# A graph layer and 64 routed experts on one core: aggregation turned round, a third output buffer, gate and up products side by side

## What is computed

```python
h = layernorm(x)
agg = segment_sum(h[src], dst)
t = relu(batch_norm(((1 + eps) * h + agg) @ W1 + b1))
x = x + h + relu(batch_norm(t @ W2 + b2))
y = layernorm(x)
shared = sum(swiglu(y, sWg[e], sWu[e], sWd[e]) for e in range(2))
gate = normalised top 6 of softmax(y @ Wr)
routed = sum(swiglu(y, Wg[e], Wu[e], Wd[e]) * gate[:, e:e+1] for e in range(64))
out = x + y + shared + routed
```

## Time and profile before

| | us |
|---|---|
| median of 3 runs (782.78 to 783.72) | 783.21 |
| the profiled execution | 782.4 |
| its span, first to last instruction | 780.7 |
| PE busy (7096 products) | 722.4 |
| DVE busy | 260.5 |
| ACT busy | 195.1 |
| POOL busy | 174.7 |
| HBM read and written, over the span | 301 GB/s |

### The profile page before, as it was taken

How to read it: one execution, slowest core, us unless ns; L and a number is a source line. 1 busy time by engine, 2 the same in 40 slices (tenths; PEclk the granted TensorE clock), 3 DMA queues, 4 the chain that set the end, 5 groups by cost and what they waited for, 6 DMA issues and landing times. The chain is left out here.

```text
span 780.7 us, 17521 instructions
## 1 busy us (share of the span) xinstructions
PE 722.4 (93%) x7096; PEld 478.5 (61%) x7096; DVE 260.5 (33%) x788; ACT 195.1 (25%) x497; POOL 174.7 (22%) x157
## 2 busy tenths in 40 slices
PE   2699999879999999999999999999999999489993
PEld 2597776556666666555566666655566666356662
DVE  7983524975221442222221212121233222012100
ACT  1222321402332222211222222121222333033331
POOL 4000000011222232232332222222333332123211
PEclk9999999999999999999999999999999999789996
DMA  9970021426999999999999999999999999999921
GB/s 265 407 280 3 0 108 62 166 75 222 354 341 337 347 387 382 392 392 380 385 387 390 378 401 377 384 394 389 383 384 372 373 374 368 342 369 364 337 36 23
DMA packets 57265, 236.35 MB, mean 303 GB/s; under 512 B 6171, under 2 KB 6335, under 8 KB 40286
## 3 DMA queue, kind: packets, MB, share of 16 engines
q1 hardware_dynamic: 46004, 211.33, 70.8%
q0 software_dynamic: 10144, 20.56, 11.4%
q10 hardware_dynamic: 1034, 3.30, 1.1%
HBM read 222.32 MB, written 12.83 MB: 301 GB/s over the span
## 5 line engine op out<-in xcount | busy, mean ns | idle before, releaser
L424 POOL DMA_INDIRECT xg<-x_tab,idx_sb x64 | 71.8, 1121 | 387.9 <-DVE idx_sb L942 220.0
L1368 PE MATMUL ps<-ring,xT 128*64 128x256 f32 x1296 | 156.5, 383 | 0.6 <-ACT xT L608 0.6
L439 POOL DMA_INDIRECT out<-ysb,idx_sb x64 | 92.5, 1445 | 202.4 <-DMA out<-ysb,idx_sb 124.4
L1368 PEld LDWEIGHTS ps<-ring,xT 128*64 128x64 f32 x1296 | 88.1, 137 | 43.8 <-issue 3.4
L628 ACT ACTIVATE ysb<-ps 64x256 f32<-64x256 f32 x64 | 24.2, 377 | 332.3 <-PE ps L1368 152.5
L935 DVE TENSOR_REDUCE gates<-ps 128x1 f32<-128x3 f32 (+1 forms) x62 | 10.0, 162 | 267.7 <-PE ps L1275 267.0
L1368 PE MATMUL ps<-ring,hTj 128*64 128x256 f32 x624 | 75.5, 384 | 0.0
L1368 PE MATMUL ps<-w,xT 128*64 128x256 f32 x608 | 75.1, 390 | 0.0
L903 DVE TENSOR_TENSOR onehot<-iotaAB,slotv 125x640 bf16<-125x640 f32 (+1 forms) x64 | 67.3, 1051 | 2.6 <-PE ps L1283 1.8
L999 DVE SCALAR_TENSOR_TENSOR hs<-hs,gates,ps 128x256 f32<-128x256 f32 x64 | 30.7, 480 | 90.2 <-PE ps L1373 43.8
L1368 PEld LDWEIGHTS ps<-ring,hTj 128*64 128x64 f32 x624 | 42.1, 136 | 30.1 <-issue 11.9
(11 more groups left out here) (237 smaller groups left out, 818.2 us busy)
## 6 DMA issues: line engine op xcount, KB each, us to landing
ring<-in_L_ffn_Wg SPq DMA_DIRECT2D x41, 1024.0 KB, 20.7
ring<-in_L_ffn_Wu SPq DMA_DIRECT2D x40, 1024.0 KB, 21.2
ring<-in_L_ffn_Wd SPq DMA_DIRECT2D x39, 1024.0 KB, 22.5
w<-in_L_ffn_Wd SPq DMA_DIRECT2D x20, 1024.0 KB, 22.4
w<-in_L_ffn_Wg SPq DMA_DIRECT2D x19, 1024.0 KB, 21.6
w<-in_L_ffn_Wu SPq DMA_DIRECT2D x19, 1024.0 KB, 21.3
ring_x<-in_L_ffn_Wu SPq DMA_DIRECT2D x5, 1024.0 KB, 20.2
ring_x<-in_L_ffn_Wd SPq DMA_DIRECT2D x5, 1024.0 KB, 20.3
```

The source lines that it names most:

```text
L424: g.indirect_dma_start(out=xg[j % NX][0:ROWS[j], :], out_offset=None, in_=x_tab, in_offset=bass.IndirectOffsetOnAxis(ap=idx_sb[0:ROWS[j], ...
L439: g.indirect_dma_start(out=out, out_offset=bass.IndirectOffsetOnAxis(ap=idx_sb[0:ROWS[j], j:j + 1].bitcast(u32), axis=0), in_=ysb[h][0:ROW ...
L1368: last = t_.matmul(ps[h * BIG:(h + 1) * BIG, bank, 0:AW], big(k), w[:, k, h * AW:(h + 1) * AW], start=(k == 0), stop=(k == KD - 1))
```

## The change

In the graph stage:

- The operands of the aggregation change places: aT is stationary and h0 moving, so a block's result comes out as rows, 125 x 512, in one PSUM bank. Both are of type float32r; h0 is held as a rounded part h0_hi (ACT) and the rest h0_lo (DVE), and both parts are multiplied: 10 products of 512 columns a block.
- at_diag and agg_copy go. Instead DVE computes h rows = (1 + eps) h0 + PSUM (`h_rows`), PE transposes them (4 products), and ACT copies to hT (blocks 0 to 3) or DVE adds onto zeros (block 4).
- The destination column is spread to int16 by ACT, one activation of 125 x 625 a group, up to ten groups ahead (`spread`); DVE's one_m then has int16 in, int16 in and bf16 out.
- The memory for this is that of ring slots 4 to 7, so SP issues the fifth weight tile only when hT is complete.

In the expert stage:

- Three ysb buffers, one semaphore for all scatters; y_copy(j) waits for scatter(j - 3).
- BASE_AFTER is 47.
- For j >= 1 the gate and up products come together, ahead of transposes, slot product and shared unit; for wide positions the four parts are gate 64, up 64, gate 32, up 32. `tiled`, still used for down, has the 32-row part first.
- The slot values of the experts from 6 on are filled in (`fill_slots(FIXED, E)`) ahead of the sort instead of behind it.

```diff
-    BASE_AFTER = 50
+    BASE_AFTER = 47
+    NY = 3
+    NREP = 10
@@ sync
+                if i == 4:
+                    sp.wait_ge(s_hT, T)
@@ gpsimd: scatter
                 pool.wait_ge(s_y, j + 1)
-                if j >= 2:
-                    pool.wait_ge(s_scat[h], j // 2 * 16)
                 if j >= 1:
-                    pool.wait_ge(s_scat[1 - h], (j + 1) // 2 * 16)
+                    pool.wait_ge(s_scat, 16 * j)
@@ scalar
+            def spread(b):
+                for g in range(b * GB, (b + 1) * GB):
+                    if g >= NREP:
+                        act.wait_ge(s_sm, g - NREP + 1)
+                    sc.activation(rep[g % NREP][:], col_m[:, g * U:(g + 1) * U].unsqueeze(2).broadcast_to([P, U, P]),
+                                  ACT.Copy).then_inc(s_rep, 1)
...
             for t in range(T):
+                sc.activation(h0_hi[:, t, :], x_sb[:, t, :], ACT.Identity, bias=negm[:, t:t + 1],
+                              scale=rstd[0:P, t:t + 1]).then_inc(s_hi, 1)
                 sc.activation(h0[:, t, :], x_sb[:, t, :], ACT.Identity, bias=negm[:, t:t + 1],
                               scale=rstd[0:P, t:t + 1]).then_inc(s_h0, 1)
-            act.wait_ge(s_pre, PRE)
             block_copy(1)
+            spread(2)
             for b in range(2, T):
-                agg_copy(b - 2)
+                if b + 1 < T:
+                    spread(b + 1)
                 block_copy(b)
+                if b == 2:
+                    act.wait_ge(s_pre, PRE)
+                hT_copy(b - 2)
+            hT_copy(T - 2)
@@ vector
+                    last = v.tensor_tensor(one_m[slot][:], iota_m[:], rep[g % NREP][:], ALU.is_equal)
...
+            def h_rows(b):
+                dve.wait_ge(s_agg, b + 1)
+                if b >= 2:
+                    dve.wait_ge(s_hrT, b - 1)
+                v.scalar_tensor_tensor(hrow[b % 2][:], h0[:, b, :], eps1[:], ps[0:P, 4 + b % 2, :], ALU.mult,
+                                       ALU.add).then_inc(s_hrow, 1)
+            block_onehots(1)
+            for t in range(T):
+                dve.wait_ge(s_hi, t + 1)
+                dve.wait_ge(s_h0, t + 1)
+                v.tensor_tensor(h0_lo[:, t, :], h0[:, t, :], h0_hi[:, t, :].bitcast(f32), ALU.subtract).then_inc(s_lo, 1)
+            for b in range(2, T):
+                block_onehots(b, 0, 2)
+                h_rows(b - 2)
+                block_onehots(b, 2, GB)
+            h_rows(T - 2)
+            h_rows(T - 1)
@@ tensor
-            def aggregate(from_aT, bank):
-                for d in range(KD):
-                    for s in range(T):
-                        last = t_.matmul(ps[:, bank, d * P:(d + 1) * P], h0[:, s, d * 128:(d + 1) * 128],
-                                         from_aT[:, s, :], start=(s == 0), stop=(s == T - 1))
+            def aggregate(from_aT, bank, done):
+                for s in range(T):
+                    for part in (h0_hi, h0_lo):
+                        last = t_.matmul(ps[0:P, bank, :], from_aT[:, s, :], part[:, s, :],
+                                         start=(s == 0 and part is h0_hi), stop=(s == T - 1 and part is h0_lo))
...
+            block_aggregate(0)
             for b in range(2, T):
-                block_aggregate(b - 2)
                 visits(b)
-            block_aggregate(T - 2)
+                block_transposes(b - 2)
+                block_aggregate(b - 1)
+            block_transposes(T - 2)
             block_aggregate(T - 1)
...
+            def gate_and_up(x, w_gate, w_up, j):
+                last = big_tiles(0, lambda k: x[:, k, 0:BIG], w_gate())
+                if CAPS[j] == BIG:
+                    last.then_inc(s_g, 1)
+                pe.wait_ge(s_mul, j)
+                if CAPS[j] > BIG:
+                    big_tiles(1, lambda k: x[:, k, 0:BIG], w_up())
+                    small_tiles(0, lambda k: x[:, k, BIG:CAP], w_gate()).then_inc(s_g, 1)
+                    small_tiles(1, lambda k: x[:, k, BIG:CAP], w_up()).then_inc(s_u, 1)
+                else:
+                    big_tiles(1, lambda k: x[:, k, 0:BIG], w_up()).then_inc(s_u, 1)
```

More of the change, by code:

```diff
@@ L161, in gnn_moe_kernel @@
         ring_x = rH0.place("ring_x", [128, KD, 512], f32)
-        aT = [rAT.place(f"aT{i}", [P, T, P], f32) for i in range(2)]
+        aT = [rAT.place(f"aT{i}", [P, T, P], f32r) for i in range(2)]
+        iota_m = rAT.place("iota_m", [P, U, P], i16)
+        hrow = [rAT.place(f"hrow{i}", [P, D], f32) for i in range(2)]
+        rep = [rAT.place("rep0", [P, U, P], i16)]
         rAT.rewind()
@@ L199, in gnn_moe_kernel @@
         hTj = rWin.place("hTj", [128, HW], f32)
-        ysb = [rWin.place(f"ysb{i}", [CAP, D], f32) for i in range(2)]
+        ysb = [rWin.place(f"ysb{i}", [CAP, D], f32) for i in range(NY)]
         perm = rWin.place("perm", [E, E], f32)
@@ L203, in gnn_moe_kernel @@
         keyd = rWin.place("keyd", [E, E], f32)
-        cntL = rWin.place("cntL", [E, 128], f32)
-        numL = rWin.place("numL", [E, 128], f32)
         orderB = rWin.place("orderB", [128, E], f32)
         cntS = rWin.place("cntS", [128, E], f32)
-        ring = [rOh.place(f"ring{i}", [128, KD, 512], f32) for i in range(8)]
+        ring = [rOh.place(f"ring{i}", [128, KD, 512], f32) for i in range(4)]
+        upper = rOh.at
+        ring += [rOh.place(f"ring{4 + i}", [128, KD, 512], f32) for i in range(4)]
+        past = rOh.at
+        rOh.at = upper
+        h0_hi = rOh.place("h0_hi", [P, T, D], f32r)
+        h0_lo = rOh.place("h0_lo", [P, T, D], f32r)
+        rep += [rOh.place(f"rep{i}", [P, U, P], i16) for i in range(1, NREP)]
+        assert rOh.at <= past
+        rOh.at = past
         w2 = [rOh.place(f"w2_{i}", [128, KD, 512], f32) for i in range(2)]
@@ L277, in gnn_moe_kernel @@
         s_go = sem("indirect_let_through")
-        s_scat = [sem(f"y_added{i}") for i in range(2)]
+        s_scat = sem("y_added")
         s_base = sem("base_added")
@@ L657, in _ @@
                     h_copy(o + E, AW)
-                    y_copy(o + E, 0, o + E // 2, BIG)
+                    y_copy(o + E, 0, o + E, BIG)
         @block.vector
@@ L700, in columns, with group_onehots @@
                 return v.tensor_tensor(col_m[:], ps[0:P, 6, 256:256 + NV], grp_of[:], ALU.subtract)
-            def group_onehots(g, slot):
+            def group_onehots(g, slot, spread):
                 c = slice(g * U, (g + 1) * U)
-                for one, iota, col in ((one_s, iota_s, col_s), (one_m, iota_m, col_m)):
-                    last = v.tensor_tensor(one[slot][:], iota[:].unsqueeze(1).broadcast_to([P, U, P]),
-                                           col[:, c].unsqueeze(2).broadcast_to([P, U, P]), ALU.is_equal)
+                v.tensor_tensor(one_s[slot][:], iota_s[:].unsqueeze(1).broadcast_to([P, U, P]),
+                                col_s[:, c].unsqueeze(2).broadcast_to([P, U, P]), ALU.is_equal)
+                if spread:
+                    last = v.tensor_tensor(one_m[slot][:], iota_m[:], rep[g % NREP][:], ALU.is_equal)
+                else:
+                    last = v.tensor_tensor(one_m[slot][:], iota_m[:], col_m[:, c].unsqueeze(2).broadcast_to([P, U, P]),
+                                           ALU.is_equal)
                 last.then_inc(s_sm, 1)
@@ L1036, in _ @@
             slot_onehot(4)
+            fill_slots(FIXED, E)
             sort_keys()
@@ L1040, in _ @@
             unit(*unit_at[0])
-            fill_slots(FIXED, E)
             take_sorted()
@@ L1440, in _ @@
                     extra_spread()
-                if j >= 1:
-                    pe.wait_ge(s_mul, j)
-                gate_up(1, xT[h], weights(1, j), s_u, CAPS[j])
+                if not both:
+                    if j >= 1:
+                        pe.wait_ge(s_mul, j)
+                    gate_up(1, xT[h], weights(1, j), s_u, CAPS[j])
                 if j == 0:
```

146 lines of the change are left out of this document (86 added, 60 removed).

## The result

The changed kernel takes **775.6 us** (median of 19 runs, 771.6 to 782.9) against 783.2 for the kernel before beside it (19 runs, 779.2 to 786.2). The ratio is 0.991 with an interval of 0.989 to 0.993: faster by 7.6 us in the medians, by 5 to 9 over the interval. The forecast was 767 with a range of 757 to 779: the sign and the range hold, the size is a little under half of what was expected. The profiled execution took 780.4 (span 778.6), 4.7 above its median, so this trace shows more lost time than a middle run.

A forecast was written before the change was run, and what follows sets the result against it. PE's order of work sets the pace, with the weight stream and POOL's serial scatters close behind. Gains of 1.4, 3.0 and about 4 us, then a smaller base hole and the scatter chain, gave span 764.9 (-15.8), forecast 767, range 757 to 779.

The forecast's parts named there:

- the graph stage: Stage before the experts: W1 starts at 62.0 instead of 63.4, a gain of 1.4 us.
- the wide positions: Expert stage: the new order has 4 array changes instead of 7, saving 0.5 us at each of 22 positions.
- "2.3 us": Graph stage: a block's turned aggregation takes 10 products of 0.23 us; only the first runs at the lower clock, 4.5 us.
- my rival with 12%: Graph stage: PE idles half of it, so aggregations stay at the lower clock, 2.3 us more on four; total 777, chance 0.12.
- nearly all that DVE wins is given back in waits: Graph stage: DVE's cheaper one-hots are mostly offset by waiting at h_rows for the aggregation, leaving W1 1.4 us earlier.
- Narrow positions: Expert stage: 23 positions with a shared unit lose two array changes, 5.8 us; about 4 expected along the scatter chain.
- First six positions: Start of the expert stage: the six wide first positions gain 3.0 us from the new order of products.
- The base, from 17.2 to 10: PE's hole behind the base DMA: about 6 us idle and 4 for half clock, instead of 17.2 us.
- each released by the landing of the one before: Sign at the kernel's end: scatters 48 to 59 each wait for the previous scatter's landing.
- the terms behind it: Expert stage: first positions 3.0, scatters 6 to 47 about 4, and the base's hole from 17.2 to 10 us.
- 0.90 on faster: Whole kernel: chance 0.90 that the change is faster by more than about 0.2%; same 0.03, slower 0.07.

The follow-up runs named there:

- a2: The kernel before with the new graph stage alone, everything else as before; 785.0 us, ratio 1.004 to the kernel before.
- b4: The changed kernel with 45 added products that nobody reads, in PE's waits in the graph stage and from 160 to 180 us; 771.4 us, ratio 0.985.
- a3: The changed kernel with two y buffers and the base after scatter(50), as in the kernel before; 782.1 us, ratio 0.999.
- a1: The changed kernel run again as it is; 774.4 us, ratio 0.989 to the kernel before.
- c2: The changed kernel with h_rows behind a block's fourth group instead of second, plus the added products that nobody reads; 766.7 us, ratio 0.979.
- c3: The changed kernel with the base as two DMAs of 64 and 61 partitions, after scatter(47) and scatter(52); 840.5 us, ratio 1.074.
- b1: The changed kernel with the base after scatter(58) instead of scatter(47); 771.7 us, ratio 0.985.
- b2: The changed kernel with the base after scatter(60) instead of scatter(47); 778.0 us, ratio 0.993.

## Why the prediction was wrong, step by step

Two terms of the sum failed: the graph stage, which the forecast put at -1.4 us with every later aggregation at full clock and which came out at +1.5 to +3.0, and the wide positions, 0.5 us each, which gave 0.25 to 0.3. They carry 4.5 to 6 us of the 8.6 that are missing; the cause of the rest stays open.

- **Graph stage, -1.4: wrong, +1.5** in a2's median, +3.0 by its ratio. The single prices held: one_m 0.39 (forecast 0.43), turned product 0.23 (0.23), block by block 7.45 us in b4 (7.3), the wait at h_rows 1.12 (0.9). At full clock W1 starts at 63.3 (62.0), and 1.0 of that is in the tail, which takes 9.6 us in b4 (8.6). The step that failed is "2.3 us" for every aggregation but the first, with visits at full clock: in the change's profile the four later ones take 3.2, 2.4, 3.7 and 2.4 us, as the clock falls twice, and W1 starts at 66.3. That was my rival with 12%, and I wrote down its mechanism rightly: PE idle because DVE can't feed it. It came half way: the mean clock of the stage lies anywhere from 0.76 to 1.00, though PE's longest idle time in the rows of the block above is 1.38 us. The Trainium skill ("TensorE: Matmul & The Clock Gate", the section on why this matters for your kernels) warns of gaps between bursts; by it I gave the rival its chance. The trace agrees that the slow clock comes back, but the gaps are short ones. Of the 3.0 us between 63.3 and 66.3, 1.4 are DVE's longer wait at h_rows for the aggregation of which four products ran slow, which passes PE's delay on to the engine that bounds the stage, and 1.6 are a slower tail.
- **The same step, seen the other way**: "nearly all that DVE wins is given back in waits" was true and should have raised the question where h_rows stands. Behind four groups (4.4 us) it waits 0.21 us even for the slow first aggregation. That place is worth 6 to 7 us, as much as each other part of the change, and most of it (5.0 us) at full clock too.
- **Narrow positions, 5.8: right.** gate(6) to gate(46) takes 345.6 us; it took 351.3.
- **First six positions, -3.0: wrong, -1.4, and not kept in this execution.** From the first gate product of position 0 to that of position 6 it takes 63.0 us in the profile of before, 61.6 in b4 at full clock and 64.6 in that of after, where half clock from 175.1 to 181.9 takes it back.
- **Wide positions, 0.5 each: 0.25 to 0.3.** They are 9.4 us apart where PE waits for nothing, from 9.65 to 9.71 (forecast 9.15). The six products themselves take 0.44 less, nearly the forecast; what the sum left out is PE idle ahead of the down product, 0.1 to 0.64 us: only transposes and a slot product lie between the transposes of hs and it, and the copy of hTj no longer has the up product as cover. That was read off the trace, no run was made for it.
- **The base, from 17.2 to 10: right.** gate(52) to gate(53) is 17.9 where 9.4 is usual, so 8.5; a3 prices base and buffer at 7.7 us. The second idle stretch went with the third buffer. Scatters follow at 9.3 us (9.1). The sign "each released by the landing of the one before" is only half there: from scatter(48) on the profile names a landing as what ended the wait of 3 of 16 and y_copy for one, and nothing for 12; but y_copy on ACT itself waits for a scatter's landing seven times there, 30.6 us in all.
- **The sum.** Against the profiled 778.6 the forecast span of 764.9 misses 13.7 us: 4.3 until W1, 0.1 until gate(0), 4.5 until gate(6) (3.0 of it the half clock, 1.6 the price of wide positions), 1.0 until scatter(47), 2.1 from there to scatter(48), 1.2 to scatter(63) and 0.5 behind it. In the median it is 8.6 us (775.6 against 767). Run against run (a1, a2), the graph stage is short by 2.9 us in the medians or 4.4 by the ratios, and the terms behind it, forecast at 14.2 together, bring 10.6 or 11.9, short by 3.6 or 2.3; the wide first positions are 1.6 of that, and for the rest no run gives a cause. With the two faults cured (c2) the kernel takes 766.7, just the 767 of the forecast, but not for its reasons: W1 then starts 3.7 us earlier than I had it, and the rest is later by as much.
- **Chances.** 0.90 on faster was right. The range of 757 to 779 held because the rival of the slow clock was in it: 775.6 is nearer to that rival's 777 than to the forecast.

## What to carry to other kernels

When a faster instruction thins out another engine's work, take the price of what follows at both clock levels, and ask on which queue a late result is waited for. An instruction that needs another engine's result belongs as late in its queue as its own readers allow: here two groups further back cost nothing and started the next stage 5.0 us earlier at full clock. Where two cures meet at one serial point (an earlier PE, a third buffer), price each with and without the other before adding them up, and compare with the spread of the runs.

## What was not expected of the hardware

- A DMA of 61 partitions took 72.2 us, one of 64 partitions 14.8 us (c3), with accumulation into the output; the mean DMA share was 0.07 while little else moved.
- The same base took 18.6 us of the chain after scatter(58) (b1) and 12.2 after scatter(60) (b2).
- Products that nobody reads made the kernel 3 to 4 us faster (b4), and its four runs agree within 2.1 us where the nineteen of the change spread over 11 and the six of a1 over 9.5.
- The same kernel's W1 started between 66.3 and 68.7 us in two executions: stretches at half clock in a thinly filled stage differ from one execution to the next, and with them the time.
- POOL's last drain took 10.5 us in the kernel without the base, 1.0 to 2.3 in the others.
